# Expert tiles of 352 slots instead of 256 in a mixture-of-experts block on one Trainium2 core

## What is computed

```
x = x + tanh(g_xattn[0]) * xattn(layernorm(x), ctx_1024, Wq, Wkv)
z = layernorm(x)
probs = softmax(z @ gate_w + gate_b, axis=1)          # over the 256 tokens of a batch
vals, idx = top_k(probs, 2)                           # two of 8 experts for each token
h = relu(z @ w1[e] + b1[e]); h = relu(h @ w2[e] + b2[e]); y = relu(h @ w3[e] + b3[e])
v[e] = sum over the tokens of e of y * weight         # one vector of 512 for each expert
x = x + tanh(g_ffn[0]) * (sum of v[e] over the token's two experts)
```

## Time and profile before

| | |
|---|---|
| median of 3 runs | 1046.24 us |
| the profiled execution | 1047.99 us, its span 1046.2 us |
| mean granted TensorE clock | 0.978 of full speed |
| PE, DVE, POOL, ACT busy | 95%, 82%, 52%, 48% of the span |
| instructions | 23915 |
| moved by DMA | 111.46 MB, 107 GB/s on average |

### The profile page before, as it was taken

The page is one execution under the profiler, slowest core; times in us unless marked ns, Lnnn a source line. Parts: engine busy times, 40 slices in busy tenths (PEclk is TensorE's granted clock), DMA queues, the critical chain, the costliest instruction groups (busy, mean ns, idle before and its releaser), DMA issues.

```text
span 1046.2 us, 23915 instructions
## 1 busy us (share of the span) xinstructions
PE 999.0 (95%) x7580; PEld 949.5 (91%) x7580; DVE 856.9 (82%) x1653; ACT 503.1 (48%) x752; POOL 543.5 (52%) x442
## 2 busy tenths in 40 slices
PE   5999999999999798999999999999999999999975
PEld 4999989989998798999999999999999999999961
DVE  6567888788788888788888888888888888888865
ACT  4354444444334644545555555555545555555511
POOL 1224444444544674556647566564756657466423
PEclk9999999999999898999999999999999999999995
DMA  6333323323214322344444432322331132232008
GB/s 211 142 115 110 100 81 119 121 80 120 100 61 141 112 59 85 117 148 152 146 131 151 130 121 54 120 68 56 96 110 41 42 129 71 91 121 53 21 12 321
DMA packets 57763, 111.46 MB, mean 107 GB/s; under 512 B 26368, under 2 KB 26624, under 8 KB 52992
## 3 DMA queue, kind: packets, MB, share of 16 engines
q1 hardware_dynamic: 50080, 92.60, 26.8%
q0 software_dynamic: 7648, 18.42, 6.3%
HBM read 93.89 MB, written 17.10 MB: 106 GB/s over the span
## 4 chain that ended last, share of the span: by engine, by line
PE 88%; DVE 6%; issue 2%; POOL 1%; ACT 1%; DMA 0%; POOLq 0%; DVEq 0%; SPq 0%; ACTq 0%
PE bank L1185 27%; PE bank L1186 26%; PE bank L1187 26%; PE bank L1199 4%; DVE w_lo L810 1%; PE bank L1434 1%; PE bank L1248 1%; PE bank L1275 1%; POOL h_lo L586 0%; PE bank L1210 0%; PE bank L1277 0%; DVE x_all L900 0%; DMA wk_raw<-in_wk_t 0%; PE bank L1212 0%; PE bank L1211 0%
## 5 line engine op out<-in xcount | busy, mean ns | idle before, releaser
L586 POOL TENSOR_TENSOR h_lo<-h,h_hi 128x512 fp32r<-128x512 f32 x140 | 253.4, 1830 | 248.4 <-DVE h_hi L1061 248.4
L810 DVE TENSOR_TENSOR w_lo<-w_raw,w_hi 128x2048 fp32r<-128x2048 f32 x105 | 284.9, 2713 | 67.0 <-ACT w_hi L725 60.6
L1185 PE MATMUL bank<-h_hi,w_hi 128*128 128x256 f32 x1104 | 316.7, 287 | 9.3 <-POOL h_lo L586 5.0
L1186 PE MATMUL bank<-h_lo,w_hi 128*128 128x256 f32 x1104 | 313.7, 284 | 0.0
L1187 PE MATMUL bank<-h_hi,w_lo 128*128 128x256 f32 x1104 | 313.6, 284 | 0.0
L725 ACT ACTIVATE w_hi<-w_raw 128x2048 fp32r<-128x2048 f32 x105 | 201.0, 1915 | 116.8 <-PE bank L1187 116.8
L1185 PEld LDWEIGHTS bank<-h_hi,w_hi 128*128 128x128 f32 x1104 | 213.1, 193 | 16.0 <-issue 15.9
L1186 PEld LDWEIGHTS bank<-h_lo,w_hi 128*128 128x128 f32 x1104 | 213.2, 193 | 0.0
L1187 PEld LDWEIGHTS bank<-h_hi,w_lo 128*128 128x128 f32 x1104 | 213.1, 193 | 0.0
L733 ACT ACTIVATE h<-bank,bias 128x256 f32<-128x256 f32 x280 | 117.7, 472 | 192.5 <-PE bank L1187 191.6
L1185 PE MATMUL bank<-et_hi,w_hi 128*128 128x256 f32 x560 | 158.8, 284 | 0.8 <-DVE x_all L900 0.7
(11 more groups left out here) (192 smaller groups left out, 1815.7 us busy)
## 6 DMA issues: line engine op xcount, KB each, us to landing
w_raw<-in_w SPq DMA_DIRECT2D x36, 1024.0 KB, 4.9
wb<-slot_pair SPq DMA_DIRECT2D x35, 256.0 KB, 3.1
xt_raw<-in_x_t SPq DMA_DIRECT2D x16, 512.0 KB, 4.1
x_all<-in_x SPq DMA_DIRECT2D x16, 512.0 KB, 4.9
c_raw<-in_ctx_t SPq DMA_DIRECT2D x16, 512.0 KB, 3.3
xn_dram<-xn SPq DMA_DIRECT2D x16, 512.0 KB, 3.0
out<-x_all SPq DMA_DIRECT2D x16, 512.0 KB, 5.4
bias<-in_b SPq DMA_DIRECT2D x105, 2.0 KB, 1.6
```

The lines of the kernel that those rows point to most:

```text
L586: pool.tensor_tensor(h_lo[n][:, 2 * k:2 * k + 2], h[n][:, 2 * k:2 * k + 2], h_hi[n][:, 2 * k:2 * k + 2].bitcast(F32), ALU.subtract).then_i ...
L810: dve.tensor_tensor(dst, src, hi.bitcast(F32), ALU.subtract).then_inc(done, 1)
L1185: pe.matmul(out_ap, lh, rh, start=(i == 0), stop=False)
L1186: pe.matmul(out_ap, lh, rl, start=False, stop=False)
```

## The change

A tile has 352 slots, gathered and transposed in chunks of 128, 128 and 96 rows. An expert's region has 12 tiles (4224 slots) in place of 4096. The number of tiles of an expert, which was a shift by 8, is now counted by comparing the count with the multiples of 352 (`count_tiles`). One output chunk of 128 takes a PSUM bank of its own, so a layer takes four banks: layer 2 takes banks 0 to 3, layers 1 and 3 take banks 4 to 7, the transposes take banks 0, 1 and 2 (the first tiles have their own lists). `h` is one buffer for both layers; `h_hi` and `h_lo` stay two. Several buffers of the attention and of the experts change places in SBUF.

```
-TILE = 256
-TH = TILE // P
+TILE = 352
+CHUNKS = [(a, min(P, TILE - a)) for a in range(0, TILE, P)]
+TH = len(CHUNKS)
-REGION = TOK
+TILES_MAX = -(-TOK // TILE)
+NT_MIN = -(-TOK * TOPK // TILE)
+REGION = TILES_MAX * TILE
...
-            h = [alloc(ph, f"h{n}", [P, DC, TILE], F32) for n in range(2)]
+            h = alloc(ph, "h", [P, DC, TILE], F32)
...
-        bL = [[bank[0], bank[3]], [bank[4], bank[5]], [bank[6], bank[7]]]
-        bZ = [bank[6], bank[7], bank[0], bank[3]]
-        bT = [bank[1], bank[2]]
+        def layer_banks(n, m):
+            first = {(0, 0): (0, 1, 2, 3), (0, 1): (4, 5, 6, 2), (1, 0): (2, 3, 0, 1)}
+            own = (0, 1, 2, 3) if n == 1 else (4, 5, 6, 7)
+            return [bank[b] for b in (first.get((n, m), own) if isinstance(m, int) else own)]
+        def row_banks(m):
+            first = {0: (1, 2, 0), 1: (4, 5, 6), 2: (3, 0, 1)}
+            return [bank[b] for b in (first.get(m, (0, 1, 2)) if isinstance(m, int) else (0, 1, 2))]
...
-                sp.dma_start(idx[:].rearrange("p h a -> p (h a)"),
-                             slot_pair[bass.ds(r, TILE)].rearrange("(p h) a -> p (h a)", p=P)
-                             ).then_inc(idx_in, 16)
+                for c, (first, rows) in enumerate(CHUNKS):
+                    sp.dma_start(idx[0:rows, c], slot_pair[bass.ds(r + first, rows)]).then_inc(idx_in, 16)
...
-                for t in range(TH):
-                    pool.indirect_dma_start(xg[:, t], None, rows,
+                for c, (_, n) in enumerate(CHUNKS):
+                    pool.indirect_dma_start(xg[0:n, c], None, rows,
...
+            def relu_half(n, m, k):
+                act.wait_ge(l_done[n], 2 * m + k + 1)
+                if n == 0:
+                    need(act, h_los[1], 2 * (m - 1) + k + 1)
+                else:
+                    need(act, h_los[0], 2 * m + k + 1)
...
             split_w(1, 0)
-            relu(0, 0)
+            act.wait_ge(b_in[0], 16)
+            relu_half(0, 0, 0)
             norm2(B - 1)
+            relu_half(0, 0, 1)
             et_high(1)
...
             def layer1_half(m, k):
-                need(pe, relu_done[0], DC * m)
+                    need(pe, part_done, m - 1)
...
-            def layer2_half(m, k):
+            def layer2_half(m, k, left=AHEAD + 1):
+                    need(pe, et_los, TH * (m + (2 if has_tile(1, left) else 1)))
+                    need(pe, relu_done[1], DC * m)
...
             def layer3_half(m, k):
-                need(pe, part_done, m)
+                need(pe, relu_done[0], DC * (m + 1) + (3 if k == 0 and isinstance(m, int) and m == 0 else 2 + 2 * k))
...
             xn2_transposes(B - 2)
             need(pe, qa_los, 2 * B)
-            row_transposes(0)
+            row_transposes(0, range(2))
             gate_logits(B - 2)
+            row_transposes(0, range(2, TH))
             p_times_v(B - 1)
             layer1_half(0, 0)
```

More of the change, by code:

```diff
@@ L245, in flamingo_block @@
             acc = alloc(ph, "acc", [P, DC], F32)
+            h_hi1 = alloc(ph, "h_hi1", [P, DC, TILE], F32R)
+            h_lo1 = alloc(ph, "h_lo1", [P, DC, TILE], F32R)
+            h_hi, h_lo = [h_hi0, h_hi1], [h_lo0, h_lo1]
             w_hi, w_lo = [w_hi0, w_hi1, w_hi2], [w_lo0, w_lo1, w_lo2]
@@ L842, in gt_low @@
                     need(dve, gt_his, 2 * m + k + 1)
-                    low(gt_lo[:, 2 * k:2 * k + 2], two(bG[k]), gt_hi[:, 2 * k:2 * k + 2], gt_los)
+                    low(gt_lo[:, 2 * k:2 * k + 2], two(gate_banks(m)[k]), gt_hi[:, 2 * k:2 * k + 2], gt_los)
             def slots(m, parity):
@@ L988, in do @@
                     link(ins, early_step, step)
[L990 to L993, removed]
+                count_tiles(do, ntile[:], TILE)
                 tile_list(do, 0, EARLY, ntile[:, 0:E - 1])
@@ L1058, in h_high, with weighted_sum @@
                 need(dve, l_done[n + 1], 2 * m)
+                if n == 1 and isinstance(m, int) and m == 0:
+                    dve.wait_ge(gate_done, B)
                 for k in range(2):
                     dve.wait_ge(relu_done[n], DC * m + 2 * k + 2)
-                    dve.tensor_copy(h_hi[n][:, 2 * k:2 * k + 2], h[n][:, 2 * k:2 * k + 2]).then_inc(h_his[n], 1)
+                    dve.tensor_copy(h_hi[n][:, 2 * k:2 * k + 2], h[:, 2 * k:2 * k + 2]).then_inc(h_his[n], 1)
             def et_low(m):
-                for k in range(2):
-                    dve.wait_ge(et_his, 2 * m + k + 1)
-                    low(et_lo[:, 2 * k:2 * k + 2], two(bT[k]), et_hi[:, 2 * k:2 * k + 2], et_los)
-            def weighted_sum(m, left=AHEAD):
+                for c, (a, n) in enumerate(CHUNKS):
+                    dve.wait_ge(et_his, TH * m + c + 1)
+                    low(et_lo[:, :, a:a + n], row_banks(m)[c][:, 0:DC * n].rearrange("p (c s) -> p c s", c=DC),
+                        et_hi[:, :, a:a + n], et_los)
+            def weighted_sum(m):
                 dve.wait_ge(b_in[2], 16 * (m + 1))
@@ L1141, in tile @@
                 if has_tile(0, left):
-                    weighted_sum(j, left)
+                    weighted_sum(j)
             tiles = tiles_in_use(dve)
@@ L1254, in xn2_transposes @@
                 need(pe, gt_los, 2 * m)
-                transpose_rows(xn2, bG, tg_done)
+                if isinstance(m, int) and m == B - 1:
+                    need(pe, relu_done[0], 2)
+                transpose_rows(xn2, gate_banks(m), tg_done)
             def x_times_a(m):
@@ L1367, in layer3_by_parts, with row_transposes @@
                             last.then_inc(l_done[2], 1)
-            def row_transposes(m):
+            def row_transposes(m, chunks=range(TH)):
                 need(pe, gathered, 16 * TH * (m + 1))
-                need(pe, et_los, 2 * m)
-                transpose_rows(xg, bT, te_done)
+                for c in chunks:
+                    n = CHUNKS[c][1]
+                    if isinstance(m, int) and m == 0:
+                        need(pe, pt_los, B if c == 2 else 0)
+                    elif isinstance(m, int) and m == 1:
+                        need(pe, x2_done, RC * B)
+                        need(pe, gt_los, 2 * (B - 1))
+                    elif isinstance(m, int) and m == 2:
+                        need(pe, relu_done[1], 2 + c)
+                    else:
+                        need(pe, relu_done[1], DC * (m - 2) + c + 1)
+                    for dc in range(DC):
+                        last = pe.transpose(row_banks(m)[c][:, dc * n:(dc + 1) * n], xg[0:n, c, dc * P:(dc + 1) * P],
+                                            ident[0:n, 0:n])
+                    last.then_inc(te_done, 1)
             scores(B - 1)
@@ L1404, in tile @@
                 if has_tile(0, left):
-                    layer2_half(j, 0)
-                    layer2_half(j, 1)
+                    layer2_half(j, 0, left)
+                    layer2_half(j, 1, left)
                 if has_tile(1, left):
```

100 lines of the change are left out of this document (56 added, 44 removed).

## The result

The changed kernel takes **982.48 us** (median of 4 runs, 982.17 to 983.4) against 1046.07 us for the kernel before (4 runs, 1045.27 to 1047.45). The ratio is **0.9392, 95% interval [0.9379, 0.9404]**. The forecast was 991.7 us: the sign and the mechanism hold, the time lies in the range, and the forecast is 9.2 us too high. The profiled execution took 983.4 us, its span 981.6.

The account below looks back on a forecast made before the run. PE's instructions were taken to bound the expert loop. Loop -72.0, start +16.4 and end +1.0 sum to -54.6 us, so the median becomes 991.7 us; the range is 976 to 1013 us.

Parts of the forecast that it names:

- left over at the loop's turn: Steady expert loop: 0.30 us of each period beyond matmuls and transposes, placed at the loop's turn and kept in the 24.7.
- `et_lo` ends, layer 2 starts: Steady loop, e being the end of layer 1 of tile j+1: `et_lo` ready 1.4 us before PE's next layer 2.
- last matmul to final transposes: Kernel's end: four weighted sums on DVE, one after the other, each grow by about 0.25 us: +1.0 us.
- fewer tiles: Expert loop: 24 tiles instead of 35, 8448 columns for each product instead of 8960, 3456 matmuls instead of 5040.
- the price as a line: PE's matmuls: 0.422 ns a column between the paces at 256 and 512 columns, so 160.5 ns for 352.
- the rival with a threshold: PE's matmuls: 352 columns priced like 512, 228.1 ns, 234 us more, about 1225 us; chance 0.05 (slower).
- The rival with 25 tiles: Expert 5, with exactly 1056 places, gets one token more and needs a fourth tile: 1016 us; chance 0.07.
- the waits at the end that were kept: From tile 4's transposes to the last matmul: 1.4 us of waits at the end, carried over unchanged.
- 0.69 to 0.94: Weighted sums on DVE: each of the four grows from 0.69 to 0.94 us with the slots.
- The start: Tiles 0 to 3: transposes of tile 4 come at 439.1 us instead of 422.67, +16.4 us; bounds 431 and 447.
- the walk: Start followed layer by layer: added matmuls, new waits for `ranks` and `et_lo`, and the `h_lo` wait almost wholly gone.
- The rival with `et_lo` in every tile: Steady loop: layer 2 waits for DVE's `et_lo` in every tile, 1 us in 20 tiles: 1012 us; chance 0.12.

Follow-up runs that it names:

- The kernel before with the plain sums: Kernel before, tiles still 256, `idx` loaded by chunks so the weighted sum reads its weights in order: 1036.23 us, ratio 0.9906.
- one and two pads: Changed kernel with one or two unused DVE reductions over 1024 columns ahead of `et_low` in the loop: 981.64 us (ratio 0.9401) and 1006.17 us (0.9634).

## Why the prediction was right, and where it was off

| step | forecast | measured |
|---|---|---|
| tiles | 24 | 24 |
| a matmul of 352 columns | 160.5 ns | 160.0 ns |
| transposes of a tile | 1.30 us | 1.21 us |
| left over at the loop's turn | 0.30 us | none |
| period | 24.7 us | 24.27 us |
| transposes of tile 4 | 439.1 | 441.00 |
| `et_lo` ends, layer 2 starts | e + 7.9, e + 9.3 | e + 7.2, e + 8.9 |
| `h_lo` | 2.5 us | 1.78 us |
| a weighted sum | 0.94 us | 0.59 us |
| last matmul to final transposes | 6.0 us | 4.0 us |

**Right: fewer tiles, and the price as a line.** Three widths between 256 and 512 columns lie on it within 0.5 ns, so the rival with a threshold is out. The rival with 25 tiles did not come. That the gain comes with the size is shown by the run at 256 slots, with the two terms below that cancel there.

**Wrong: "the 0.30 us left over lies at the loop's turn".** This was the step of the working that failed. The text took a remainder and gave it a cause without a row, then carried it into the new period as a constant. It was PE's wait at layer 3 for POOL's second `h_lo`, which a strided read in the sums had pushed behind `w_lo`. It is gone in the changed kernel, where the sums read in order and a layer of 7.68 us covers more; which of the two would be enough was not tried. From the transposes of tile 4 to the last matmul the forecast was 9.5 us too high (516.7 + 1.4 against 508.6). Of that 18 x 0.30 = 5.4 are this term, 20 x 0.09 = 1.8 the transposes, whose 96-row chunks were not credited, 63 x 48 x 0.5 ns = 1.5 the pace; the rest, 0.8, lies among the waits at the end that were kept.

**Wrong in size: the sums.** "0.69 to 0.94" scaled a duration of which part was the access pattern: 493 ns instead of 687 for the same 256 columns. The diff removes the rearrangement of `wb`, and the forecast did not price that. At the end this is 2 us: four sums start 0.69 us apart instead of 0.76, where 0.25 us more each were forecast, and a wait of 0.5 us ahead of the last small steps of DVE is gone. The kernel before with the plain sums still has that wait, so the sums are not its reason; no run shows what is.

**The start** came 1.9 us later than forecast, and executions of the same start code differ by more than that. Four were profiled: the transposes of tile 4 came at 441.0 and 440.4 (the changed kernel, twice) and at 434.7 and 435.0 (with one and two pads). Counted from the POOL step near 320 us they are 14.4 to 18.6 us longer than before, where 16.4 was forecast. One piece can be named: in the two later ones DVE stands for 1.9 us ahead of one small step, for which the profile names no engine of this core; the two others and the kernel before do not have this wait.

```profile
335.66 0.69 DVE L846 TENSOR_REDUCE smax<-bank 128x2 f32<-128x512 f32 x1 [1.95 <-remote]
```

So no step of the walk is shown wrong by the 1.9 us, and none is shown right by it: of the waits forecast there, that for `et_lo` of tiles 2 and 3 (1 and 1.7 us) shrank to 0.2 in all, and that for the ranks grew. The late start also hid part of the 9.5 us of the loop, so that the sum is off by less than its largest term; that is luck.

**The rival with `et_lo` in every tile** had the right mechanism and the right distance: a margin of 1.4 us was forecast and 1.7 measured; 1.2 us more fit, 2.5 don't. It comes true at 256 slots. There the change's other parts cancel: the plain sums give about 10 us, and as much goes again. Against the kernel before with the plain sums, 7.0 us of it lie between the transposes of tiles 4 and 34, which is this wait at 0.25 us a period, and 3.9 us before them (425.01 against 421.15); those were not taken apart. So of the 63.6 us against the kernel before some 54 are left against the best kernel of 256 slots that was run (ratio 0.9392 against 0.9906); the other 10 belong to a stall that could be removed without changing the size. 352 slots with the strided sums were not tried.

## What to carry to other kernels

When a period computed from paces leaves a remainder, however small, look for the instruction that starts late and follow its operands back, before the remainder is carried on as overhead: read starts, since a wait of 0.3 us is missing from the list of waits. A tile size that leaves fewer empty slots and needs fewer instructions pays by both counts, and longer layers also cover more of the chain beside them; take the pace at two widths and draw the line. Time saved on an engine that is not the bound can still be worth much, where it decides which of two instructions that hold each other up starts first.

## What the runs showed of the hardware

- **The order in which a second input is read costs on DVE.** The weighted sum of 256 columns takes 687 ns with its weights read four floats apart in two passes, 493 ns with the same weights two floats apart in one; 352 columns in that order take 593. The edit also took the split in two passes out of the sum's first input and output, and no run separates the two.
- **The time from one fp32r matmul with its own weight load to the next is a line in the columns:** 120.0, 133.1, 160.0, 173.7 and 228.1 ns for 256, 288, 352, 384 and 512 columns at a granted clock of 1.00, 0.42 ns a column plus about 12 to 13 ns.
- **The order in which DVE and POOL start moves the cost from one to the other:** `h_lo` 2.68 and `w_lo` 3.19 us, or `h_lo` 4.69 and `w_lo` 2.68, for the same two pieces and one `w_lo`; two pieces that meet no `w_lo` take 2.6.
- **Short waits of PE don't show as idle time.** 0.31 us in a period of the kernel before, 0.22 in one of the changed kernel at 256 slots, and 0.16 of 1.04 with the two pads are absent from the list of waits and show in the starts alone.
